# Token mixer of an audio tower: lead of the first scores, order of transfers and adds, and the queue of a third of the stacking transfers

## The chip, the cores and the metric

The kernel runs on one core of a Trainium2 chip. The metric is the device time of one execution in microseconds (us). TensorE, VectorE, ScalarE and GpSimd compute; SyncE and ScalarE also issue the transfers, each on a queue of its own.

## The reference, cut to what matters

The program is a token mixer and two layers of attention and feed-forward. Only the mixer is changed. It is an attention over the 512 time steps of each of 128 sequences, with 32 channels:

```python
q, k, v = jnp.split(qkv, 3, axis=1)                    # 128 sequences, 32 channels, 512 steps
weight = jnp.einsum('bct,bcs->bts', q * scale, k * scale)
weight = jax.nn.softmax(weight.astype(jnp.float32), axis=-1).astype(weight.dtype)
h = jnp.einsum('bts,bcs->bct', weight, v)
```

## The kernel before

The mixer (`token_mixer`, lines 73 to 504) works through 32 tiles of four sequences. Inputs are split into two float16 parts (line 318 on ScalarE, the high part; line 268 on GpSimd, the low part), and stacked in three groups of 32 partitions into `tm_qk`, so that one matmul over 96 rows gives scores of full precision. The stacking is done by transfers within the chip: `stack`, line 207, three for each of the four sequences, on SyncE's queue.

Scores are computed twice. The **first scores** (line 426, bank `tm_s1`, three banks) serve only for the maximum of each row: VectorE reduces them (line 371), and after eight such reductions TensorE transposes the maxima (line 434), VectorE splits them in two float16 rows (lines 381 and 383), and two small transfers (line 214, `maxima`) put these rows under the stacked inputs. The **second scores** (line 446, `tm_s2`, two banks of two) then have the maximum subtracted inside the matmul. ScalarE takes their exponential (line 330, eight for a tile, each over the scores of two places). GpSimd (line 283, three of four sequences) and VectorE (line 397, the last) add halves of the exponentials, TensorE sums these over the rows (line 479, `sum_probs`, into bank 2 of `tm_s1`) and multiplies the exponentials with the values (line 460, `sum_values`). ScalarE copies both out (lines 338 and 344). The sums are brought to a dense shape by a transfer (line 223, `denominators`), inverted on VectorE (line 390), spread again by way of DRAM (lines 230 and 237), and multiplied in on GpSimd (line 275).

All engines follow an order written out by hand. A step n has 16 places g, and at each place TensorE does one first score, of a tile ahead, and one second score of tile n. `LEAD = 15` says how many places the first scores run ahead: at place g stands number g + 15. `MAXIMA_AT` gives the places of the transposes (11 for the first half of the next tile, 3 for the second half of this one; their rows are used at places 0 and 8), `VALUES_AT` those of the four blocks of values (14, and 0, 2, 4 of the next step), `SUMS_AT` those of the two blocks of sums of the tile before (8 and 10). `BANK` names the bank of each use of `tm_s1`: while the sums of a tile hold bank 2, only banks 0 and 1 alternate. Semaphores count each of these; a second score of exponential i waits for exponential i - 2 (`exp_done`), since they share a bank. Steps 4 to 27 are a loop of two steps, the others are written out, the last ones between steps of the attention (`mixer_into_attention`).

Of the kernel before, what the change touches and what calls it, by code (L numbers as in the profile page):

```python
# [72 lines left out]
def token_mixer(nc, sb, ps, sem, qk_dram, vt_dram, ident_dram, rden_dram, h_dram, SEQS=128):  # L73
    C, T = 32, qk_dram.shape[2]
    P = 128
# [11 lines left out]
    LEAD = 15  # L87
# [56 lines left out]
    MAXIMA_AT = {11: 0, 3: 1}  # L144
    VALUES_AT = {14: (0, 0), 0: (1, 1), 2: (1, 2), 4: (1, 3)}
    SUMS_AT = {8: 0, 10: 1}
# [49 lines left out]
    def sync(sp):  # L196
# [3 lines left out]
        def stack(t, u, b):  # L200

            if inside(t, TILES):
                wait_alone(sp, sp_passed, xlo_done, t + 1)
                wait_alone(sp, sp_passed, s2_ready, 8 * (t - 2) + 4 * (b // 2) + 4)
                c = slice(b * C, (b + 1) * C)
                for g, (lo, hi) in enumerate(((0, 2), (0, 3), (1, 2))):
                    sp.dma_start(qk[u][g * C:(g + 1) * C, :, b, :],
                                 xs[u][c, lo:hi + 1:hi - lo, :]).then_inc(stacked[u][b], 16)
# [8 lines left out]

        def denominators(t, u):

            if inside(t, TILES):  # L220
                wait_alone(sp, sp_passed, sums_out, t + 1)
                wait_alone(sp, sp_passed, rden_done, t - 1)
                sp.dma_start(dens[u][:, :], nd[u][0:P:C, 1, :].rearrange("b (a e) -> b a e", e=E))\
                    .then_inc(dens_in[u], 16)
# [18 lines left out]
        def step(k, u):  # L243
            n = 2 * k + u
            stack(n + 1, 1 - u, 2)
            stack(n + 1, 1 - u, 3)
            inverses(n - 2, u, k - 1)
            maxima(n, u, 1)
            inverse_rows(n - 2, u, k - 1)
            stack(n + 2, u, 0)  # L250
            stack(n + 2, u, 1)
            maxima(n + 1, 1 - u, 0)
            denominators(n - 1, 1 - u)
# [10 lines left out]
    def gpsimd(pool):  # L264
# [21 lines left out]
        def step(k, u):  # L286
            n = 2 * k + u
            add(n - 1, 2)
            x_lo(n + 3, 1 - u)
            if not isinstance(n, int) or n < TILES:  # L290
                normalise(n - 2, u, k - 1)
            add(n, 0)
            add(n, 1)
        return step, normalise

    def scalar(act):
        def load(t, u):
            if inside(t, TILES):
                wait_alone(act, act_passed, xlo_done, t - 1)
                act.dma_start(xqk[u][:, :, :], qk_dram[bass.ds(t * P, P)]).then_inc(qk_in[u], 16)  # L300

# [43 lines left out]

        def step(k, u):
            n = 2 * k + u
            for i in range(8):
                exps(n, i)
                if i == 2:  # L350
                    copy_values(n - 1, 1 - u, k + u - 1)
                    load_values(n + 1, 1 - u)
                if i == 3:
                    x_hi(n + 3, 1 - u, k + 1 + u)
                if i == 4:
                    copy_sums(n - 1, 1 - u)
                    load(n + 4, u)
                if i == 6:
                    store(n - 2, u)
        return step, copy_values, copy_sums  # L360

    def vector(dve):
# [37 lines left out]
        def step(k, u):  # L400
            n = 2 * k + u
            for g in range(SLOTS):
# [5 lines left out]
                if g == 1:  # L408
                    inverse_sums(n - 2, u, k - 1)
                if g == 3:  # L410
                    add_last(n - 1)
        return step, inverse_sums, add_last
# [734 lines left out]
def mixer_into_attention(nc, ctx, mixer, att, ternary, down, beside, beside_scalar, beside_vector, beside_tensor,  # L1147
# [66 lines left out]
    def _(act):  # L1214
        mix, copy_values, copy_sums = mixer.scalar(act)
# [21 lines left out]
        copy_sums(31, 1)  # L1237
        run(step, -1, 0)
# [9 lines left out]
    def _(dve):  # L1248
# [14 lines left out]
        inverse_sums(30, 0, 15)  # L1263
        statistics, normalised, low, _, _ = ternary.vector(dve)
        for n in range(1, 34):
            step(n // 2, n % 2, statistics, normalised, low)
            if n == 1:
                inverse_sums(31, 1, 15)
            beside_vector(dve, n)
# [1424 lines left out]
```

## Time and profile before

| what | value |
|---|---|
| median of 3 runs | 2353.75 us (2352.59 to 2357.39) |
| the profiled execution | 2357.19 us, span 2355.4 us |
| granted clock of TensorE, mean | 0.985 of 2.4 GHz |
| busy over the whole span | TensorE 94%, VectorE 71%, ScalarE 65%, GpSimd 54% |
| busy from 100 to 500 us | TensorE 359.3 of 400 us, VectorE 298.0, ScalarE 249.0, GpSimd 253.9; transfer engines 48% |

The mixer takes the first 550 us. Each row of a timeline gives the start of an instruction (or of some alike in a row, x their number), its recorded length, and in brackets how long its engine had been idle and what ended that. Matmuls overlap, so that start to start tells more of TensorE than their length.

### The profile page before, as it was taken

The page shows a single profiled execution, that of the slowest core. Times are in us where ns is not written, and L with a number is a line of the kernel's source. Part 1 is how long each engine was busy: PE and PEld are TensorE (multiplying, and loading weights), DVE is VectorE, ACT ScalarE, POOL GpSimd, SP SyncE. Part 2 cuts the span into 40 slices and gives each one's busy share as a digit, 9 for nine tenths or more (in the row PEclk, how much of TensorE's full clock was granted, in tenths as well). Part 3 has the DMA queues.
Part 4 walks back from the last instruction along what each step waited for, and adds up shares of the span by engine and source line. Part 5 has one row for each costly group of instructions (what it writes and reads, how often), then busy time and mean ns, then how long its engine had stood idle before and what let it go on. Part 6 is the DMA issues. An engine that isn't in the chain of part 4 may idle for free. (4 is left out here: it accounts for less than half of the span.)

```text
span 2355.4 us, 42715 instructions
## 1 busy us (share of the span) xinstructions
PE 2202.6 (94%) x13828; PEld 1076.9 (46%) x13828; DVE 1674.3 (71%) x2922; ACT 1524.0 (65%) x2430; POOL 1266.6 (54%) x1141
## 2 busy tenths in 40 slices
PE   6889889987899998899999999999998999999997
PEld 1222222223566665444444444666664444444443
DVE  6777777774777979666666743666666787788875
ACT  4656666666678779446555522766675777777775
POOL 4566666667677778332324401444444566666654
PEclk9999999998999999899999999999999999999999
DMA  5444454441334222312222212222221011111111
GB/s 147 132 130 133 124 137 125 130 129 38 91 128 132 76 68 68 102 51 79 79 85 85 81 49 72 73 80 79 79 84 46 27 51 50 41 50 41 41 36 63
DMA packets 144049, 194.99 MB, mean 83 GB/s; under 512 B 30469, under 2 KB 73957, under 8 KB 143898
## 3 DMA queue, kind: packets, MB, share of 16 engines
q1 hardware_dynamic: 115866, 154.79, 22.0%
q10 hardware_dynamic: 28032, 38.28, 5.3%
q8 instruction: 84, 1.38, 0.2%
q14 instruction: 67, 0.55, 0.1%
HBM read 125.10 MB, written 42.21 MB: 71 GB/s over the span
## 5 line engine op out<-in xcount | busy, mean ns | idle before, releaser
L2294 PE MATMUL f_bank<-f_xs,gu 128*128 128x512 f16 x1408 | 417.2, 379 | 1.5 <-ACT f_firstg L2120 0.8
L371 DVE TENSOR_REDUCE tm_negmax<-tm_s 128x1 f32<-128x512 f32 x512 | 323.1, 673 | 95.2 <-PE tm_s L426 94.6
L330 ACT ACTIVATE tm_prob<-tm_s 128x1024 f32<-128x1024 f32 x256 | 261.1, 1024 | 192.1 <-PE tm_s L446 173.9
L2322 PE MATMUL f_bank<-dn,f_ghi 128*128 128x512 f16 x704 | 265.6, 379 | 1.9 <-DVE f_glo L2229 1.9
L426 PE MATMUL tm_s<-tm_qk 96*128 96x512 f16 x512 | 200.6, 394 | 47.7 <-DVE tm_negmax L371 27.7
L2084 POOL TENSOR_TENSOR f_firstg<-f_firstg,f_secondg 128x512 f32<-128x512 f32 x88 | 152.2, 1729 | 152.8 <-DVE f_secondg L2213 152.8
L283 POOL TENSOR_TENSOR tm_added<-tm_prob 128x1024 f32<-128x1024 f32 x96 | 223.7, 2355 | 2.3 <-PE tm_s L479 2.2
L446 PE MATMUL tm_s<-tm_qk 98*128 98x512 f16 x512 | 198.0, 389 | 22.6 <-DMA tm_qk<-tm_mrow 19.9
L2294 PEld LDWEIGHTS f_bank<-f_xs,gu 128*128 128x128 f16 x1408 | 136.0, 98 | 162.7 <-ACT f_firstg L2120 1.3
L268 POOL TENSOR_TENSOR tm_xs<-tm_xqk,tm_xs 128x1024 f16<-128x1024 f32 x32 | 68.2, 2130 | 189.9 <-ACT tm_xs L318 189.9
L1048 PE MATMUL a_bankB<-a_wo,a_yThi 128*128 128x512 f16 x512 | 158.7, 393 | 0.0
L2084 POOL TENSOR_TENSOR f_firstu<-f_firstu,f_secondu 128x512 f32<-128x512 f32 x88 | 123.9, 1408 | 64.5 <-DVE f_secondu L2213 64.5
L1088 PE MATMUL a_bankB<-a_wqkv,a_xhi 128*128 128x512 f16 x512 | 154.3, 383 | 0.2
L426 PEld LDWEIGHTS tm_s<-tm_qk 96*128 96x128 f16 x512 | 49.9, 98 | 228.0 <-DVE tm_negmax L371 139.0
L1576 POOL TENSOR_TENSOR fw_value<-fw_value,fw_code 128x512 f32<-128x512 f32 (+1 forms) x35 | 43.8, 1252 | 184.1 <-DVE fw_value L1529 177.3
L460 PE MATMUL tm_o<-tm_prob,tm_vt 128*32 128x512 f32 x1024 | 141.4, 626 | 0.0
L1910 PE MATMUL f_pz<-tern,f_ghi 128*128 128x512 f16 (+1 forms) x352 | 134.4, 382 | 2.9 <-DVE f_glo L1795 2.9
L1910 PE MATMUL f_pz<-tern,f_glo 128*128 128x512 f16 (+1 forms) x352 | 134.2, 381 | 0.0
L2322 PE MATMUL f_bank<-dn,f_glo 128*128 128x512 f16 x352 | 133.4, 379 | 0.0
L698 POOL TENSOR_TENSOR a_qs<-a_qkv,a_qs 128x512 f16<-128x512 f32 x32 | 37.0, 1156 | 171.8 <-ACT a_qs L817 171.8
L748 ACT COPY a_qT<-a_bankD 128x512 f16<-128x512 f16 x128 | 68.6, 587 | 86.2 <-PE a_bankD L1021 86.2
L674 POOL TENSOR_TENSOR a_crossed<-a_qkv,a_sin 128x64 f32<-128x64 f32 (+1 forms) x128 | 80.5, 648 | 73.6 <-ACT a_qkv L787 73.6
(197 smaller groups left out, 5770.1 us busy)
## 6 DMA issues: line engine op xcount, KB each, us to landing
tm_qk<-tm_xs SPq DMA_DIRECT2D x384, 64.0 KB, 2.4
tm_xqk<-in_qk ACTq DMA_DIRECT2D x32, 512.0 KB, 3.8
a_hin<-h SPq DMA_DIRECT2D x64, 256.0 KB, 2.7
a_hres<-h SPq DMA_DIRECT2D x64, 256.0 KB, 3.0
h<-a_hout SPq DMA_DIRECT2D x64, 256.0 KB, 2.5
f_hin<-h SPq DMA_DIRECT2D x64, 256.0 KB, 2.9
f_hres<-h SPq DMA_DIRECT2D x64, 256.0 KB, 2.9
tm_vt<-in_vt ACTq DMA_DIRECT2D x32, 256.0 KB, 6.0
```

The source lines that it names most:

```text
L283: pool.tensor_tensor(added[b][:, :, :], prob[b][:, 0:2, :], prob[b][:, 2:4, :], ALU.add)\
L330: nc.scalar.activation(prob[b][:, 2 * h:2 * h + 2, :], s2[:, i % 2, :, :], ACT.Exp, scale=SCALE).then_inc(exp_done, 1)
L371: nc.vector.tensor_reduce(negmax[u][:, m:m + 1], s1[:, BANK[p], :], AX.X, ALU.max, negate=True).then_inc(s1_read, 1)
L426: nc.tensor.matmul(s1[:, BANK[place(m)], :], qk[u][0:KS, 0, b, i * P:(i + 1) * P], qk[u][0:KS, 1, b, :], start=True, stop=True).then_inc(s ...
L446: last = nc.tensor.matmul(s2[:, i % 2, j, :], qk[u][0:KM, 1, b, s:s + P], qk[u][0:KM, 0, b, :], start=True, stop=True)
L460: last = nc.tensor.matmul(o[C * b:C * (b + 1), :], vt[u][:, j, :, b], prob[b][:, j, :], start=j == 0, stop=j == NT - 1)
L1048: last = nc.tensor.matmul(bankB[:, :], a, w[:, r, :], start=n == 0, stop=n == 3 * R - 1)
L1088: last = nc.tensor.matmul(out, a[u][:, j, :], w[:, j, cols], start=n == 0, stop=n == 3 * KT - 1)
L1910: last = nc.tensor.matmul(pz[i % 2][:, :], gparts[x][u][0:rows[m], m, i * P:(i + 1) * P], down[0:rows[m], m, :], start=c == 0, stop=c == 2 ...
L2084: pool.tensor_tensor(to[:, :], to[:, :], other[:, :], ALU.add).then_inc(s["sum_done"], 1)
L2294: last = nc.tensor.matmul(bank_of(m, i)[:, :], (gate, up)[which][:, j, m * P:(m + 1) * P], xs[g % 2][:, x, j, :], start=x == 0, stop=x == 1)
L2322: last = nc.tensor.matmul(pz[i][:, :], gparts[x][:, (MT * g + m) % RING, i * P:(i + 1) * P], down[w][:, m, :], start=m == 0 and c % 3 == 0 ...
```

## The change

- `LEAD` goes from 15 to 17. The transposes move with it, from places 11 and 3 to 9 and 1, the sums from places 8 and 10 to 5 and 7; VectorE's add (line 397) goes from behind place 3 to behind place 2, and its reciprocal (line 390) from place 1 of the step after next to place 14 of the next.
- The third stacking transfer of each sequence (`stack_last`) is issued by ScalarE: those of two sequences behind the first exponential of a step, those of two behind the fifth.
- The transfer of the denominators is issued by ScalarE too, right behind the copy of the sums, which moves from behind the fifth exponential to behind the fourth. The high part of the inputs (`x_hi`, line 318) moves from behind the fourth to behind the fifth.
- GpSimd makes the low part of the inputs (`x_lo`) at the end of a step and no longer before its multiplication and two adds.
- SyncE's order is a new one, below. At the end of the mixer the last denominators and reciprocals follow the new order.

```diff
-    LEAD = 15
+    LEAD = 17
...
-    MAXIMA_AT = {11: 0, 3: 1}
+    MAXIMA_AT = {9: 0, 1: 1}
     VALUES_AT = {14: (0, 0), 0: (1, 1), 2: (1, 2), 4: (1, 3)}
-    SUMS_AT = {8: 0, 10: 1}
+    SUMS_AT = {5: 0, 7: 1}
...
-                for g, (lo, hi) in enumerate(((0, 2), (0, 3), (1, 2))):
+                for g, (lo, hi) in enumerate(((0, 2), (0, 3))):
...
             n = 2 * k + u
             stack(n + 1, 1 - u, 2)
+            inverse_rows(n - 2, u, k - 1)
+            maxima(n, u, 1)
             stack(n + 1, 1 - u, 3)
-            inverses(n - 2, u, k - 1)
-            maxima(n, u, 1)
-            inverse_rows(n - 2, u, k - 1)
             stack(n + 2, u, 0)
+            maxima(n + 1, 1 - u, 0)
             stack(n + 2, u, 1)
-            maxima(n + 1, 1 - u, 0)
-            denominators(n - 1, 1 - u)
+            inverses(n - 1, 1 - u, k + u - 1)
...
             add(n - 1, 2)
-            x_lo(n + 3, 1 - u)
             if not isinstance(n, int) or n < TILES:
                 normalise(n - 2, u, k - 1)
             add(n, 0)
             add(n, 1)
+            x_lo(n + 3, 1 - u)
...
+        def stack_last(t, u, b):
+
+            if inside(t, TILES):
+                wait_alone(act, act_passed, xlo_done, t + 1)
+                wait_alone(act, act_passed, s2_ready, 8 * (t - 2) + 4 * (b // 2) + 4)
+                c = slice(b * C, (b + 1) * C)
+                act.dma_start(qk[u][2 * C:3 * C, :, b, :], xs[u][c, 1:3, :]).then_inc(stacked[u][b], 16)
...
             for i in range(8):
                 exps(n, i)
+                if i == 0:
+                    stack_last(n + 1, 1 - u, 2)
+                    stack_last(n + 1, 1 - u, 3)
+                if i == 4:
+                    stack_last(n + 2, u, 0)
+                    stack_last(n + 2, u, 1)
                 if i == 2:
                     copy_values(n - 1, 1 - u, k + u - 1)
                     load_values(n + 1, 1 - u)
                 if i == 3:
+                    copy_sums(n - 1, 1 - u)
+                    denominators(n - 1, 1 - u)
+                if i == 4:
                     x_hi(n + 3, 1 - u, k + 1 + u)
-                if i == 4:
-                    copy_sums(n - 1, 1 - u)
+                if i == 5:
                     load(n + 4, u)
-                if i == 6:
                     store(n - 2, u)
...
                 maxes(n + ahead, (u + ahead) % 2, m)
-                if g == 1:
-                    inverse_sums(n - 2, u, k - 1)
-                if g == 3:
+                if g == 2:
                     add_last(n - 1)
+                if g == 14:
+                    inverse_sums(n - 1, 1 - u, k + u - 1)
```

ScalarE, a step behind its third exponential, before. `tm_prob` are the exponentials, `tm_nd` the copies of values and sums:

```order
30 L338 COPY tm_nd<-tm_o 128x512
31 L306 DMA tm_vt<-in_vt 128x4x128
32 L330 ACTIVATE tm_prob<-tm_s 128x1024
33 L318 CAST tm_xs<-tm_xqk 128x2x512
34 L330 ACTIVATE tm_prob<-tm_s 128x1024
35 L344 COPY tm_nd<-tm_s 128x512
36 L300 DMA tm_xqk<-in_qk 128x1024
37 L330 ACTIVATE tm_prob<-tm_s 128x1024 x2
38 L165 DMA h<-tm_nd 128x512
39 L330 ACTIVATE tm_prob<-tm_s 128x1024
```

And now, the same stretch, with the lines of the changed kernel:

```order
43 L337 COPY tm_nd<-tm_o 128x512
44 L305 DMA tm_vt<-in_vt 128x4x128
45 L329 ACTIVATE tm_prob<-tm_s 128x1024
46 L343 COPY tm_nd<-tm_s 128x512
47 L350 DMA tm_dens<-tm_nd 128x1x16
48 L329 ACTIVATE tm_prob<-tm_s 128x1024
49 L299 DMA tm_qk<-tm_xs 32x2x512 x2
50 L317 CAST tm_xs<-tm_xqk 128x2x512
51 L329 ACTIVATE tm_prob<-tm_s 128x1024
52 L291 DMA tm_xqk<-in_qk 128x1024
53 L165 DMA h<-tm_nd 128x512
54 L329 ACTIVATE tm_prob<-tm_s 128x1024 x2
```

The cast (318, now 317) stood between the exponentials of the long places and now stands behind two stacking transfers (299); the copy of the sums and the denominators' transfer (350) now come ahead of it.

TensorE from the second block of sums on, before, with what each instruction waits for (`tm_s1_read`: a bank read by VectorE; `tm_exp_done`: exponentials):

```order
119 L479 MATMUL tm_s<-tm_added,tm_ones 32x512 x4
120 L434 MATMUL tm_s<-tm_ident,tm_negmax 8x128 [waits tm_s1_read]
121 L426 MATMUL tm_s<-tm_qk 128x512 [waits tm_s1_read]
122 L446 MATMUL tm_s<-tm_qk 128x512
123 L426 MATMUL tm_s<-tm_qk 128x512 [waits tm_sums_out,tm_s1_read]
124 L446 MATMUL tm_s<-tm_qk 128x512 [waits tm_exp_done]
125 L426 MATMUL tm_s<-tm_qk 128x512 [waits tm_s1_read,tm_stacked13]
126 L446 MATMUL tm_s<-tm_qk 128x512
127 L426 MATMUL tm_s<-tm_qk 128x512 [waits tm_s1_read]
128 L446 MATMUL tm_s<-tm_qk 128x512 [waits tm_exp_done]
129 L460 MATMUL tm_o<-tm_prob,tm_vt 32x512 [waits tm_exp_done,tm_values_out,tm_v_in0]
130 L460 MATMUL tm_o<-tm_prob,tm_vt 32x512 x3
```

And now (line 440 is a first score, 460 a second, 448 the transpose, 493 a block of sums):

```order
115 L493 MATMUL tm_s<-tm_added,tm_ones 32x512 x4
116 L440 MATMUL tm_s<-tm_qk 128x512 [waits tm_s1_read]
117 L460 MATMUL tm_s<-tm_qk 128x512 [waits tm_exp_done,tm_mrow_in1]
118 L448 MATMUL tm_s<-tm_ident,tm_negmax 8x128 [waits tm_s1_read]
119 L440 MATMUL tm_s<-tm_qk 128x512 [waits tm_s1_read]
120 L460 MATMUL tm_s<-tm_qk 128x512
121 L440 MATMUL tm_s<-tm_qk 128x512 [waits tm_sums_out,tm_s1_read]
122 L460 MATMUL tm_s<-tm_qk 128x512 [waits tm_exp_done]
123 L440 MATMUL tm_s<-tm_qk 128x512 [waits tm_s1_read,tm_stacked13]
124 L460 MATMUL tm_s<-tm_qk 128x512
125 L440 MATMUL tm_s<-tm_qk 128x512 [waits tm_s1_read]
126 L460 MATMUL tm_s<-tm_qk 128x512 [waits tm_exp_done]
```

Before, four places (11 to 14) lie between the second block of sums and the next block of values; now seven (8 to 14, of which the rows show six and the values come after the seventh). The transpose now stands behind the first of them.

## Rows read from the trace of the kernel before

**Rows 1.** Waits from 100 to 560 us: engine and line that waited <- released by: us, times, longest.
```profile
PE tm_s L426 <- DVE tm_negmax L371: 22.5, 26, 2.1
PE tm_s L446 <- DMA tm_qk<-tm_mrow: 17.4, 23, 2.3
```
**Rows 2.** Timeline, ScalarE (start, length, operation): copy of values, first and last of 24 tiles.
```profile
111.46 0.58 ACT L338 COPY tm_nd<-tm_o 128x512 f32<-128x512 f32 x1
...
487.53 0.58 ACT L338 COPY tm_nd<-tm_o 128x512 f32<-128x512 f32 x1
```
**Rows 3.** Timeline, TensorE, one tile: start us, length, operation, [idle before it <- releaser].
```profile
317.98 1.10 PE L460 MATMUL tm_o<-tm_prob,tm_vt 128*32 128x512 f32 x8
319.01 0.39 PE L426 MATMUL tm_s<-tm_qk 96*128 96x512 f16 x1
...
324.98 0.39 PE L426 MATMUL tm_s<-tm_qk 96*128 96x512 f16 x1 [0.83 <-DVE tm_negmax L371]
...
325.81 0.38 PE L446 MATMUL tm_s<-tm_qk 98*128 98x512 f16 x1
326.12 1.06 PE L479 MATMUL tm_s<-tm_added,tm_ones 128*32 128x512 f32 x8
327.12 0.39 PE L426 MATMUL tm_s<-tm_qk 96*128 96x512 f16 x1
327.34 0.38 PE L446 MATMUL tm_s<-tm_qk 98*128 98x512 f16 x1
...
329.09 0.27 PE L434 MATMUL tm_s<-tm_ident,tm_negmax 128*8 128x128 f32 x1
329.20 0.38 PE L426 MATMUL tm_s<-tm_qk 96*128 96x512 f16 x1
...
334.00 0.39 PE L446 MATMUL tm_s<-tm_qk 98*128 98x512 f16 x1 [0.69 <-DMA tm_qk<-tm_mrow]
```
**Rows 4.** Timeline, ScalarE, the same tile (ACTq: it issues a transfer).
```profile
326.55 1.04 ACT L318 CAST tm_xs<-tm_xqk 128x1024 f16<-128x1024 f32 x1
327.84 1.02 ACT L330 ACTIVATE tm_prob<-tm_s 128x1024 f32<-128x1024 f32 x1 [0.26 <-PE tm_s L446]
329.22 0.58 ACT L344 COPY tm_nd<-tm_s 128x512 f32<-128x512 f32 x1 [0.36 <-PE tm_s L479]
329.53 0.35 ACTq L300 DMA_DIRECT2D tm_xqk<-in_qk  x1
330.05 1.99 ACT L330 ACTIVATE tm_prob<-tm_s 128x1024 f32<-128x1024 f32 x2 [0.24 <-PE tm_s L446]
```
**Rows 5.** Timeline, VectorE, the same tile.
```profile
323.66 3.06 DVE L371 TENSOR_REDUCE tm_negmax<-tm_s 128x1 f32<-128x512 f32 x5
...
327.54 1.29 DVE L371 TENSOR_REDUCE tm_negmax<-tm_s 128x1 f32<-128x512 f32 x2 [0.82 <-PE tm_s L426]
```
**Rows 6.** Timeline, SyncE's queue: a pair of row transfers, six stacking transfers.
```profile
330.17 1.45 SPq L214 DMA_DIRECT2D tm_qk<-tm_mrow  x2
...
333.19 4.03 SPq L207 DMA_DIRECT2D tm_qk<-tm_xs  x6
```
**Rows 7.** Issues by line, whole program: ns min/median/max, first and last start us.
```profile
L207 SPq DMA_DIRECT2D tm_qk<-tm_xs x384: 585/597/1772, 7.9 to 516.9; - x192
L306 ACTq DMA_DIRECT2D tm_vt<-in_vt x32: 375/395/701, 8.7 to 520.0; - x32
```
**Rows 8.** Timeline, GpSimd, one tile.
```profile
327.66 2.13 POOL L268 TENSOR_TENSOR tm_xs<-tm_xqk,tm_xs 128x1024 f16<-128x1024 f32 x1 [5.45 <-ACT tm_xs L318]
```
**Rows 9.** Timeline, TensorE: longer waits in other tiles, and a matmul behind the first.
```profile
122.14 0.60 PE L446 MATMUL tm_s<-tm_qk 98*128 98x512 f16 x1 [2.31 <-DMA tm_qk<-tm_mrow]
...
124.54 0.61 PE L426 MATMUL tm_s<-tm_qk 96*128 96x512 f16 x1
...
351.04 0.39 PE L446 MATMUL tm_s<-tm_qk 98*128 98x512 f16 x1 [1.57 <-DMA tm_qk<-tm_mrow]
...
522.43 0.39 PE L426 MATMUL tm_s<-tm_qk 96*128 96x512 f16 x1 [2.08 <-DVE tm_negmax L371]
```

More of the change, by code:

```diff
@@ L216, in maxima @@
                                  mrow[pair][:, part, :]).then_inc(mrow_in[pair], 16)
[L218 to L224, printed above, removed]
         def inverses(t, u, half):
@@ L344, in copy_sums, with denominators @@
                 nc.scalar.copy(nd[u][:, 1, :], sums_bank(t)).then_inc(sums_out, 1)
+        def denominators(t, u):
+            if inside(t, TILES):
+                wait_alone(act, act_passed, sums_out, t + 1)
+                wait_alone(act, act_passed, rden_done, t - 1)
+                act.dma_start(dens[u][:, :], nd[u][0:P:C, 1, :].rearrange("b (a e) -> b a e", e=E))\
+                    .then_inc(dens_in[u], 16)
         def step(k, u):
@@ L353, in step @@
                 if i == 3:
+                    copy_sums(n - 1, 1 - u)
+                    denominators(n - 1, 1 - u)
+                if i == 4:
                     x_hi(n + 3, 1 - u, k + 1 + u)
-                if i == 4:
-                    copy_sums(n - 1, 1 - u)
+                if i == 5:
                     load(n + 4, u)
-                if i == 6:
                     store(n - 2, u)
-        return step, copy_values, copy_sums
+        return step, copy_values, copy_sums, denominators
     def vector(dve):
@@ L1214, in _ @@
     def _(act):
-        mix, copy_values, copy_sums = mixer.scalar(act)
+        mix, copy_values, copy_sums, denominators = mixer.scalar(act)
         prepare, step = att.scalar(act)
@@ L1237, in _ @@
         copy_sums(31, 1)
+        denominators(31, 1)
         run(step, -1, 0)
@@ L1262, in _ @@
         run(step, -2, 0)
-        inverse_sums(30, 0, 15)
+        inverse_sums(31, 1, 15)
         statistics, normalised, low, _, _ = ternary.vector(dve)
@@ L1266, in _ @@
             step(n // 2, n % 2, statistics, normalised, low)
-            if n == 1:
-                inverse_sums(31, 1, 15)
             beside_vector(dve, n)
```

## The prediction

> **What bounds the kernel now.** I read the busy shares by stage first, then who waited for whom, then the timeline of one tile of the token mixer on each engine. All that changes lies in that mixer. In its steady stretch TensorE is busy some 90% of the time, ScalarE 62%, VectorE 75%, GpSimd 64% (the table above), so TensorE is the engine whose waits count. Of those two stand out [rows 1]: a first score (line 426) that waits for VectorE's maximum to free its bank, 22.5 us in 26 waits, and a second score (line 446) that waits for the small transfers of row maxima, 17.4 us in 23 waits. Rows of that list are the recorded idle time only; the tile's timeline gives the whole loss.
>
> A step has 16 places. From the same copy in 24 successive steps [rows 2]: (487.53 - 111.46) / 23 = 16.35 us a step. What TensorE needs for a step without waits [rows 3]: a place holds two matmuls 0.22 apart (327.12 to 327.34), so 0.44; a block of values adds 0.31 + 1.03 (317.98 to 319.01) less 0.22, so 1.12; a block of sums 0.31 + 1.00 less 0.22, so 1.09; a transpose 0.11 (329.09 to 329.20). The sum is 16 x 0.44 + 4 x 1.12 + 2 x 1.09 + 2 x 0.11 = 13.92 us. So 2.4 us a step are waits, and over 28 steady steps 68 us at most could be had.
>
> **The change part by part.** Times below count from the start of line 426 at place 0.
>
> *Two places more lead.* The transposes move from places 11 and 3 to 9 and 1, their users stay at 0 and 8: each row of maxima has 7 places to land where it had 5. In the tile shown it was 0.69 us late at place 0 [rows 3]; two light places are 0.88. The longest such wait was 2.31 [rows 9]. The second wait, 0.83 at place 7, came because VectorE made its own add just before (five reductions back to back, 3.06 us [rows 5]) while places 5 to 7 were short ones. After the change VectorE's add stands at place 2, among long places. Both waits go. The work of filling and draining the pipeline moves by two reductions, 2 x 0.61 us at the start, won back at the end: nothing.
>
> *What is late next.* Blocks now stand at places 0, 2, 4 (values), 5, 7 (sums) and 14 (values). Places 0 to 7 take 8 x 0.44 + 3 x 1.12 + 2 x 1.09 + 0.11 = 9.17 us. Then come six short places in a row, 8 to 13, where there were at most three. There bank 2 is lent to the sums, so only two banks alternate: place 9 needs the reduction of place 8. It starts 0.42 after its matmul (327.12 to 327.54), takes 0.63, and the bank is seen free 0.08 later (third reduction's start 323.66 + 2 x 0.61 = 324.88, second's end 324.90, matmul 324.98) [rows 3, 5]. So place 9 starts at 9.17 + 0.42 + 0.63 + 0.08 = 10.30 and not at 9.72: 0.58 us. Its second score is at 10.52, and the fifth exponential starts 0.50 behind (327.34 to 327.84) [rows 3, 4]: 11.02.
>
> *ScalarE's queue.* It gets five more issues a step: four stacking transfers and the one of denominators. An issue holds ScalarE's program: in the tile shown the load is issued from 329.53 for 0.35, and the next exponential starts at 330.05, 0.17 after it ended, as it does in other tiles [rows 4]. Issues behind the first exponential (0.31 + 1.29 + 0.17 = 1.77 us) fit before the second, 2 us later. The denominators' issue follows the copy of the sums (0.58, from 0.13 after the sums' end, 329.09 to 329.22) and waits for it: 9.17 + 0.13 + 0.58 + 0.17 + 0.60 = 10.65, before 11.02, so it is hidden. The two behind the fifth exponential are not, because the cast of the inputs (line 318, 1.04 us) follows them, and moved from the long places to just here. The nearest price of one is the same transfer on SyncE's queue, 0.597 median [rows 7], six in 4.03 us, so 0.09 between two [rows 6]. The cast starts at 11.02 + 0.31 + 0.60 + 0.09 + 0.60 + 0.17 = 12.79; the sixth exponential 1.0 later, 13.8, ends at 14.82. Place 14's second score waits for it (they share a bank of second scores): 14.90, where TensorE alone would be at 12.14 + 0.58 = 12.72. Then a block of values, 0.31 + 1.03, and place 15, 0.44: the step is 16.68 us long.
>
> Bounds of that price: from below the cheapest issue on ScalarE's queue, 0.35 [rows 4], which gives 16.18. From above an issue there while SyncE issues too: line 306 takes 0.395 and at worst 0.701 [rows 7], at 8.7 us, beside stacking transfers. SyncE's row transfers (1.45 us a pair) are issued 1.08 after their transpose (329.09 to 330.17 [rows 3, 6]), so from 10.7 at the earliest, with VectorE's reduction of place 8 ahead of its part some 10.9 to 12.4: beside the two of ScalarE's. With 0.31 more for each the step is 17.30. I add half of one, 0.15, since one overlaps wholly and the other in part: **16.83 us**.
>
> The Trainium skill (Perfetto Trace Analysis, DMA Instruction — HWDGE) says that both sequencers share one descriptor generator, and that waiting for its lock is inside the recorded issue. The longest issue of line 306 agrees with that; taken for both issues it gives the upper bound, 17.30.
>
> *SyncE, GpSimd, VectorE.* SyncE loses four of twelve stacking issues and the denominators' one, 5 x 0.60 = 3 us a step. It had room: between a pair of row transfers (to 331.62) and the next six issues (from 333.19) lie 1.57 us [rows 6], of which the denominators' took some 0.60. GpSimd's low parts move behind its two adds, in the time in which it stood idle for 5.45 us before the cast [rows 8]; its third add then ends some 2 us into the next step, where the sums want it at 5.9. The sums' earlier places need VectorE's add, over by 4.9, also in time. If either slipped by a place it would cost 0.44. The reciprocals now run at place 14, where VectorE waits anyway. Nothing for these.
>
> **Sum.** (16.83 - 16.35) x 28 = +13.4 us. The profiled execution took 2357.2 (span 2355.4), 3.4 over the median of the runs, 2353.75. The difference goes on the median: **2367 us**, slower. Without the added 0.15: +9; bounds of the issue alone: -5 to +27.
>
> **The rivals.** *Faster: the issues don't hold ScalarE.* If they are hidden behind the exponential, the cast follows at 11.02 + 0.97, the last score at 14.1, and the step is 15.88: -13 us, 2340.5. For it: all waits on rows of maxima end, and with them single ones of 1.57 and 2.31 us [rows 9]. Against: the 0.17 behind the load's issue. The Trainium skill (Trainium Kernel Development and Optimization, Key Constraints) says that issuing from several engines saves the sequencer's issue time only; here SyncE's was not on the path.
>
> *No change: losses meet gains.* With 0.40 for an issue, as line 306's median, the step is 16.28: -2 us, 2352.
>
> *Slower by more: the clock falls in the new gap.* TensorE will idle from about 13.2 to 14.9 in each step, 1.7 us, behind short waits. Before, it ran at 2.4 GHz after 1.57 and 2.08 us idle, but after 2.31 us matmuls took 0.60 (1.2 GHz) and the next first score came 2.40 us later where it should be 1.34 [rows 9]: 1.1 us lost, up to 1.5 with what follows. In half the steps that adds 14 x 1.1 to 14 x 1.5 = 15 to 21 us: 2382 to 2388. It decides once the gap exceeds some 2 us.
>
> *The change doesn't do what it says:* the order of instructions shows that it does; I give this no chance of its own.
>
> **Numbers.** A change under 0.2%, 4.7 us, can't be told from none here. Chances: the forecast 0.44 (2358 to 2380, for an issue of 0.5 to 0.9), the clock 0.16 (2380 to 2395), no change 0.14, faster 0.26 (down to 2340). Range 2340 to 2390: beyond it lie the clock falling in nearly every step, and GpSimd or VectorE freed to more than I see. Faster 0.26, same 0.14, slower 0.60.
>
> **What would show it.** Right: the step of copies near 16.8; TensorE waits at place 14 for line 329's exponential (line 330 before), 1.5 us or more, hardly ever for the row transfers, and 0.2 to 0.6 at place 9 for VectorE; each cast starts 1.7 us or more after the exponential. Wrong: a cast within 1.1 us of it, an issue of line 299 near 0.35, or a step below 16.1. For the clock: matmuls of 0.6 behind place 14 in many steps.

## The result, and the profile after

| | us |
|---|---|
| before, median of 4 runs | 2354.47 (2352.59 to 2357.39) |
| changed, median of 4 runs | 2389.24 (2386.29 to 2396.72) |
| ratio | 1.0151, 95% interval 1.0123 to 1.0179 |
| the profiled execution, changed | 2386.29, span 2384.3, granted clock 0.981 |

The change costs 34.8 us by the medians and 29.1 us by the two profiled executions (2386.29 against 2357.19). The forecast had the sign, and its range (2340 to 2390) holds the time, though by less than 1 us at its upper end; for the size it had +13.4 us.

The page of the changed kernel, its parts on the engines and on the queues, and the same stretch by windows as in the table of before (PE, PEld, DVE, ACT and POOL busy, granted clock, share of the transfer engines, GB/s):

```profile
PE 2213.5 (93%) x13828; PEld 1076.0 (45%) x13828; DVE 1677.6 (70%) x2922; ACT 1523.1 (64%) x2430; POOL 1268.7 (53%) x1141
...
q1 hardware_dynamic: 101402, 146.13, 20.1%
q10 hardware_dynamic: 42496, 46.94, 7.1%
```
```profile
100.00:500.00 400.00, 340.40 (x1830) 87.14 (x1829) 279.24 (x496) 226.61 (x249) 233.48 (x114) 0.96 0.44 118
```

Transfers have gone from SyncE's queue (q1, 22.0% of the transfer engines' time before) to ScalarE's (q10, 5.3% before), as meant. Every engine does less in the same 400 us: TensorE is busy for 340.4 us, not 359.3, and its mean clock there is 0.96, not 1.00. Nothing has become a busier engine; waits have grown, and part of the work ran at the lower clock.

Waits of TensorE from 100 to 560 us, the counterpart of [rows 1]:

```profile
PE tm_s L460 <- ACT tm_prob L329: 47.3, 26, 2.0
PE tm_s L440 <- DVE tm_negmax L385: 13.0, 28, 0.5
PE tm_s L440 <- DMA tm_qk<-tm_xs: 4.9, 9, 1.4
```

The two waits of [rows 1] are gone or halved: no row for the transfers of row maxima is left, and VectorE's 22.5 us are 13.0. In their place stands one on ScalarE's exponential, 47.3 us in 26 steps, and a new small one, on a stacking transfer.

Timeline of ScalarE, the copy of values (line 337, 338 before), five of 23, as in [rows 2]:

```profile
100.01 0.58 ACT L337 COPY tm_nd<-tm_o 128x512 f32<-128x512 f32 x1
...
245.60 0.58 ACT L337 COPY tm_nd<-tm_o 128x512 f32<-128x512 f32 x1
...
264.04 0.58 ACT L337 COPY tm_nd<-tm_o 128x512 f32<-128x512 f32 x1
...
280.87 0.58 ACT L337 COPY tm_nd<-tm_o 128x512 f32<-128x512 f32 x1
...
492.46 0.58 ACT L337 COPY tm_nd<-tm_o 128x512 f32<-128x512 f32 x1
```

The 22 steps between the first and the last take (492.46 - 100.01) / 22 = 17.84 us, 1.49 more than the 16.35 of before. But they are not alike. One takes 264.04 - 245.60 = 18.44 us, the next 280.87 - 264.04 = 16.83. Ten of the 22 lie between 18.3 and 19.9 (mean 18.77), twelve between 16.8 and 17.5 (mean 17.07).

Timeline of TensorE for another step of the shorter kind (17.37 us, since it has a wait at place 7), with its three waits (places 7, 9 and 14):

```profile
315.85 0.39 PE L440 MATMUL tm_s<-tm_qk 96*128 96x512 f16 x1 [0.31 <-DMA tm_qk<-tm_xs]
...
318.56 0.39 PE L440 MATMUL tm_s<-tm_qk 96*128 96x512 f16 x1 [0.46 <-DVE tm_negmax L385]
...
323.31 0.39 PE L460 MATMUL tm_s<-tm_qk 98*128 98x512 f16 x1 [1.91 <-ACT tm_prob L329]
323.63 1.09 PE L474 MATMUL tm_o<-tm_prob,tm_vt 128*32 128x512 f32 x8
```

Timeline of ScalarE beside it, from the fifth exponential on, the counterpart of [rows 4]:

```profile
319.29 1.02 ACT L329 ACTIVATE tm_prob<-tm_s 128x1024 f32<-128x1024 f32 x1 [1.18 <-PE tm_s L460]
319.54 1.43 ACTq L299 DMA_DIRECT2D tm_qk<-tm_xs  x2
321.29 1.05 ACT L317 CAST tm_xs<-tm_xqk 128x1024 f16<-128x1024 f32 x1 [0.98 <-PE tm_s L460]
...
322.24 1.02 ACT L329 ACTIVATE tm_prob<-tm_s 128x1024 f32<-128x1024 f32 x1
```

The chain reads off directly. The fifth exponential starts at 319.29; its two issues run to 320.97; the cast starts 0.32 after that, at 321.29, though ScalarE had been idle for 0.98 us; the sixth exponential follows at 322.24 and ends at 323.26; TensorE's second score of place 14 starts at 323.31 after 1.91 us without work. (The releaser "PE tm_s L460" of the cast is only the last semaphore seen; the cast reads nothing of TensorE. What held it are the issues.)

In a step of the longer kind the matmuls behind that gap are slow. Timeline of TensorE, the step that took 18.44 us:

```profile
253.39 0.39 PE L460 MATMUL tm_s<-tm_qk 98*128 98x512 f16 x1 [1.90 <-ACT tm_prob L329]
253.71 1.94 PE L474 MATMUL tm_o<-tm_prob,tm_vt 128*32 128x512 f32 x8
255.58 0.61 PE L440 MATMUL tm_s<-tm_qk 96*128 96x512 f16 x1
```

The block of values takes 1.94 us instead of the 1.09 at 323.63, a single matmul 0.61 instead of 0.39: the clock is at its lower level, 1.2 GHz, from 253.71 to about 257. From the gap's end to the next transpose the shown slow step takes 4.89 us (253.39 to 258.28) and an undisturbed one 3.35 (305.95 to 309.30): 1.54 us lost. There are eleven such stretches from 127 to 520 us in the mixer, where the kernel before had two in its loop, at 122 and 504 us.

### The profile page after: what moved, and what is told of

Its sections match the earlier page's. It is cut to its first block and busy times, and to the rows that moved or that the text cites. A ratio compares the mean times of both kernels' runs of the same rounds, so it can differ in the third digit from the quotient of the medians.

```text
span 2384.3 us, 42979 instructions
## 1 busy us (share of the span) xinstructions
PE 2213.5 (93%) x13828; PEld 1076.0 (45%) x13828; DVE 1677.6 (70%) x2922; ACT 1523.1 (64%) x2430; POOL 1268.7 (53%) x1141
## 5 line engine op out<-in xcount | busy, mean ns | idle before, releaser
L385 DVE TENSOR_REDUCE tm_negmax<-tm_s 128x1 f32<-128x512 f32 x512 | 328.3, 682 | 137.4 <-PE tm_s L440 134.3
L460 PE MATMUL tm_s<-tm_qk 98*128 98x512 f16 x512 | 201.8, 396 | 60.5 <-ACT tm_prob L329 57.9
L440 PE MATMUL tm_s<-tm_qk 96*128 96x512 f16 x512 | 206.3, 405 | 35.1 <-DMA tm_qk<-tm_xs 17.7
L474 PE MATMUL tm_o<-tm_prob,tm_vt 128*32 128x512 f32 x1024 | 150.6, 663 | 0.0
L266 POOL TENSOR_TENSOR tm_nd<-tm_nd,tm_rows 128x512 f32<-128x512 f32 x32 | 40.8, 1273 | 181.0 <-DMA tm_rows<-rden 181.0
```

The source lines that it names most:

```text
L385: nc.vector.tensor_reduce(negmax[u][:, m:m + 1], s1[:, BANK[p], :], AX.X, ALU.max, negate=True).then_inc(s1_read, 1)
L440: nc.tensor.matmul(s1[:, BANK[place(m)], :], qk[u][0:KS, 0, b, i * P:(i + 1) * P], qk[u][0:KS, 1, b, :], start=True, stop=True).then_inc(s ...
L460: last = nc.tensor.matmul(s2[:, i % 2, j, :], qk[u][0:KM, 1, b, s:s + P], qk[u][0:KM, 0, b, :], start=True, stop=True)
L474: last = nc.tensor.matmul(o[C * b:C * (b + 1), :], vt[u][:, j, :, b], prob[b][:, j, :], start=j == 0, stop=j == NT - 1)
```

## The experiments

Two theories at first. **A:** ScalarE's chain (fifth exponential, two issues, cast, sixth exponential) makes the gap at place 14, and the gap lets the clock fall. **B:** stacking transfers through two queues land later or disturb others, whatever ScalarE does. A third, **C:** the earlier sums and the longer lead cost time by themselves.

**The cast put back ahead (cast_back).** It runs again behind the fourth exponential, before the copy of the sums; all else as changed.

```diff
                 if i == 3:
+                    x_hi(n + 3, 1 - u, k + 1 + u)
                     copy_sums(n - 1, 1 - u)
                     denominators(n - 1, 1 - u)
                 if i == 4:
-                    x_hi(n + 3, 1 - u, k + 1 + u)
```

> The changed kernel with the cast of the inputs moved back from behind the fifth exponential (and its two stacking issues) to behind the fourth, ahead of the copy of the sums. Theory A (ScalarE's chain of fifth exponential, two issues, cast, sixth exponential holds place 14, and TensorE's clock falls in about half of the gaps this makes): the chain loses the cast, some 0.9 us; a step goes from 17.3 to 16.4 us where the clock holds, the gap at place 14 from 1.9 to about 1.0 us, the clock falls in at most two steps, and the time is 2345 to 2358 us. Theory B (the stacking transfers land later because two queues and the spread of the inverses share the transfer engines): the loss is at place 7 and stays, 2375 us or more. Theory C (the earlier sums and the longer lead cost by themselves, through the two banks): 2375 us or more.

Measured: 2370.76 us (2365.8 to 2374.78), ratio 1.0065 (1.0043 to 1.0087). 18 us better than the change, but 13 worse than I expected under A. Waits of TensorE, 100 to 560 us:

```profile
PE tm_s L459 <- ACT tm_prob L329: 35.4, 48, 0.8
...
PE tm_s L439 <- ACT tm_nd L343: 2.6, 6, 0.8
```

The one long wait has become two of at most 0.8 us a step, and of the eleven stretches at the lower clock five are left. That part of A holds. But the two waits add up to 35.4 / 24 = 1.5 us a step where 1.0 was expected, because the sixth exponential still has to wait for the two issues (it starts 1.88 us behind the fifth in the tile at 312.46). What was not foreseen is the last row, the copy of the sums, which is now late; and the waits for stacking transfers are 8.4 us in 9, up from 4.9.

**All stacking back on SyncE (on_sync).** The new order stays, ScalarE's four stacking issues go.

```diff
-                for g, (lo, hi) in enumerate(((0, 2), (0, 3))):
+                for g, (lo, hi) in enumerate(((0, 2), (0, 3), (1, 2))):
...
-                if i == 0:
-                    stack_last(n + 1, 1 - u, 2)
-                    stack_last(n + 1, 1 - u, 3)
-                if i == 4:
-                    stack_last(n + 2, u, 0)
-                    stack_last(n + 2, u, 1)
```

> The changed kernel with all three stacking transfers of a sequence on SyncE's queue again, the rest of its order kept. Theory A: the two issues (1.44 us and 0.3 behind them) go from ahead of the cast, the cast starts 0.95 us behind the fifth exponential instead of 2.0; place 14's wait falls from 1.9 to about 0.9 us, the clock holds, a step is 16.0 to 16.4 us and the time 2335 to 2355 us. Theory B: place 7's wait for stacking transfers goes too; if that alone goes, a step is shorter by 0.3 to 0.5 us and the time 2375 to 2382 us. Theory C: no change beyond 5 us, 2384 to 2394 us.

Measured: 2332.88 us (2331.99 to 2335.32), ratio 0.9914 (0.9895 to 0.9933): 56 us under the changed kernel and 22 under the kernel before, 2 us better than the range expected under A. Its step is 15.80 us in 22 steps running. The end of the gap on TensorE, then ScalarE's chain:

```profile
324.50 0.39 PE L454 MATMUL tm_s<-tm_qk 98*128 98x512 f16 x1 [0.81 <-ACT tm_prob L329]
```
```profile
321.57 1.02 ACT L329 ACTIVATE tm_prob<-tm_s 128x1024 f32<-128x1024 f32 x1 [1.18 <-PE tm_s L454]
322.49 1.04 ACT L317 CAST tm_xs<-tm_xqk 128x1024 f16<-128x1024 f32 x1
```

The cast starts 0.92 after the exponential instead of 2.00, the gap is 0.81 us, and no stretch at the lower clock is left in the loop. C falls with it: order, lead and sums' places are those of the change, and they gain 22 us.

**Both (both_back).** Cast ahead and stacking on SyncE, to see if the two repairs add up.

```diff
                 if i == 3:
+                    x_hi(n + 3, 1 - u, k + 1 + u)
                     copy_sums(n - 1, 1 - u)
...
-                    stack_last(n + 2, u, 0)
-                    stack_last(n + 2, u, 1)
```

> Both edits together: stacking all on SyncE, cast behind the fourth exponential; what is left of the change is the lead of 17, the earlier transposes and sums, the orders of SyncE, GpSimd and VectorE, and the denominators on ScalarE. Theory A: nothing but the sixth exponential itself follows the fifth, place 14 waits 0.5 us or less, a step is 15.0 to 15.6 us and the time 2318 to 2338 us, faster than both kernels. Theory B: as with stacking on SyncE alone. Theory C: not under 2354 us.

Measured: 2355.51 us (2344.21 to 2364.88), ratio 0.9998 (0.9978 to 1.0017). A miss: 23 us worse than on_sync alone. ScalarE and TensorE in one of the long steps:

```profile
331.64 1.04 ACT L317 CAST tm_xs<-tm_xqk 128x1024 f16<-128x1024 f32 x1 [0.77 <-DMA tm_qk<-tm_xs]
332.59 0.58 ACT L343 COPY tm_nd<-tm_s 128x512 f32<-128x512 f32 x1
```
```profile
333.31 0.38 PE L433 MATMUL tm_s<-tm_qk 96*128 96x512 f16 x1 [0.79 <-ACT tm_nd L343]
```

The cast overwrites the tile from which stacking transfers still read, so it waits for them to land; behind it on ScalarE stands the copy that gives bank 2 back, and for that TensorE waits: 12.1 us in 12 waits. Waits of the two engines, 100 to 560 us:

```profile
PE tm_s L433 <- ACT tm_nd L343: 12.1, 12, 2.1
```
```profile
ACT tm_xs L317 <- DMA tm_qk<-tm_xs: 13.0, 12, 3.2
```

So the cast's place is bounded from both sides. Behind the fourth exponential it is too early for the transfers, and behind the fifth with issues ahead of it too late for the sixth. Cast_back has the same waits of the cast, 3.1 us in 7, which is part of why it gained less than A said.

The waits alone are not the 23 us, though. Of the 24 steps from 98 to 494 us, the 13 without a wait for the copy take 15.4 to 15.5 us, less than the 15.80 of on_sync. Of the 11 with one, four take 16.0 to 16.4 us and seven 17.4 to 19.4 (mean 18.58), and in those seven the clock falls. TensorE in one of them:

```profile
233.77 0.38 PE L433 MATMUL tm_s<-tm_qk 96*128 96x512 f16 x1 [1.01 <-ACT tm_nd L343]
...
234.54 0.63 PE L453 MATMUL tm_s<-tm_qk 98*128 98x512 f16 x1
```

From there matmuls take 0.6 us up to 241.1. The falls cost 7 x (18.58 - 16.29) = 16 us, the larger part of the miss. And no wait of nearly 2 us stands ahead of them: in six of the seven steps the longest wait is 1.1 us or less, behind another of 0.46 at place 9. What separates them from the four steps with like waits and no fall stays open.

**A gap filled with work (gap_filled).** The first score of place 14 is computed seven times instead of once, so that some 1.3 us of the gap are busy.

```diff
+                for _ in range(6 if m == SLOTS - 1 else 0):
+                    nc.tensor.matmul(s1[:, BANK[place(m)], :], qk[u][0:KS, 0, b, i * P:(i + 1) * P],
+                                     qk[u][0:KS, 1, b, :], start=True, stop=True)
                 nc.tensor.matmul(s1[:, BANK[place(m)], :], qk[u][0:KS, 0, b, i * P:(i + 1) * P],
```

> The changed kernel with the first score of place 14 computed seven times over (the same matmul into the same bank, the last one counts), so that TensorE works for 1.3 us of the 1.9 in which it waits at place 14. The wait itself is not shortened. Theory A, its part on the clock: no stretch of 0.6 us matmuls behind place 14 in the mixer, where the changed kernel has eleven; at 1.1 to 1.3 us each the time falls by 10 to 15 us, to 2374 to 2380. If the clock were not what makes half of the steps 1.1 us longer, they stay so and the time is 2387 to 2392.

Measured: 2371.58 us (2370.26 to 2372.78), ratio 1.0075 (1.0056 to 1.0094). TensorE does 6 matmuls more in each step and the kernel is 17.7 us quicker than the changed one, somewhat more than the 10 to 15 expected. No slow stretch is left in the loop. This prices the clock apart from the gap: the second score of place 14 comes no sooner (3.97 us behind the fifth exponential's start in the tile at 327.38, 4.02 in that at 319.29 of the changed kernel), the chain on ScalarE is the same, and half of the loss goes.

**The queue alone (queue_only).** The kernel before, in its own order, with the third stacking transfers on ScalarE behind the first and the fifth exponential.

```diff
                 exps(n, i)
+                if i == 0:
+                    stack_last(n + 1, 1 - u, 2)
+                    stack_last(n + 1, 1 - u, 3)
+                if i == 4:
+                    stack_last(n + 2, u, 0)
+                    stack_last(n + 2, u, 1)
```

> The kernel before with nothing changed but the queue: the third stacking transfer of a sequence is issued by ScalarE, two behind the first exponential of a step and two behind the fifth. Theory A: behind the fifth exponential stands the copy of the sums; the two issues (1.44 us) push it 0.5 to 0.6 us later, TensorE waits that much longer at place 12, and the sixth exponential comes later too: +0.5 us in each of 28 steps, 2364 to 2374 us, the clock holds. If ScalarE's issues hurt only where the cast follows them, the time is 2350 to 2358 us.

Measured: 2356.14 us (2348.72 to 2360.71), ratio 1.0004 (0.999 to 1.0018). A miss: it costs nothing there. Waits of TensorE, 100 to 560 us:

```profile
PE tm_s L440 <- DVE tm_negmax L385: 21.1, 26, 1.3
PE tm_s L460 <- DMA tm_qk<-tm_mrow: 10.4, 22, 0.8
PE tm_s L440 <- ACT tm_nd L352: 6.3, 14, 0.5
```

In the order of before the cast stands ahead of the fifth exponential, and behind the issues there comes only the copy of the sums, for which TensorE waits up to 0.5 us (third row). That wait was expected; the loss was not there. The waits for row maxima shrink from 17.4 us [rows 1] to 10.4, though SyncE issues them no sooner behind the transpose (a median of 1.09 us in both traces). The wait for the copy stands between the transpose and the use of its rows, so that part of one wait may have taken the place of the other; this was not tried. The same transfers on the same queue cost nothing measurable here and 56 us in the new order.

**One issue instead of two (one_issue).** Of the pair behind the fifth exponential one goes back to SyncE.

```diff
                 if i == 4:
                     stack_last(n + 2, u, 0)
-                    stack_last(n + 2, u, 1)
```

> The changed kernel with one stacking issue behind the fifth exponential instead of two (that of the second sequence goes back to SyncE). Theory A: a dose. The cast starts 0.72 us earlier, place 14 waits 1.15 to 1.25 us instead of 1.9 (0.8 with none), and the clock falls in two steps at most: a step of 16.6 us where it was 17.3, and the time 2350 to 2362 us, nearer to the 2333 of none than to the 2389 of two. If it were the place of the cast alone or the sharing of queues as such, the wait would stay near 1.9 and the time above 2380 us.

Measured: 2352.65 us (2350.53 to 2356.1), ratio 0.9997 (0.9986 to 1.0008). The gap, in a typical step:

```profile
320.71 0.39 PE L459 MATMUL tm_s<-tm_qk 98*128 98x512 f16 x1 [1.07 <-ACT tm_prob L329]
...
331.18 0.39 PE L439 MATMUL tm_s<-tm_qk 96*128 96x512 f16 x1 [0.87 <-DMA tm_qk<-tm_xs]
```

From two issues to one the gap shrinks by 0.84 us, from one to none by 0.26, since most of one fits beside the exponential that ScalarE is running. At 1.07 us of gap two stretches at the lower clock are left, one at 93 us and one of 3.6 us from 471.8; the second stands in a step with waits of 0.67 and 1.12 us. The wait at place 7 (second row) stays.

**The rows of inverses later (rows_later).** That wait at place 7 is for a stacking transfer of ScalarE's first pair, issued 0.4 us behind the spread of the inverses (256 KB). Here this spread is issued behind the row maxima and the fourth stacking.

```diff
-            inverse_rows(n - 2, u, k - 1)
             maxima(n, u, 1)
             stack(n + 1, 1 - u, 3)
+            inverse_rows(n - 2, u, k - 1)
```

> The changed kernel with SyncE issuing the spread of the inverses (256 KB, the largest transfer on its queue) behind the maxima and the fourth sequence's stacking, and no longer ahead of them. Theory A takes the 0.3 to 1.4 us that place 7 waits for a stacking transfer for a transfer issued by ScalarE 0.4 us behind that spread, in line with it on the transfer engines: the wait at place 7 goes, 0.3 to 0.5 us a step, 2372 to 2382 us. Theory B (two queues by themselves make stacking land late): the wait stays, 2386 to 2392 us. A risk is the multiplication on GpSimd, which comes 3 us later and could hold back its adds.

Measured: 2401.52 us (2400.86 to 2404.82), ratio 1.0204 (1.0183 to 1.0226). A miss. Timeline of GpSimd:

```profile
303.91 1.26 POOL L266 TENSOR_TENSOR tm_nd<-tm_nd,tm_rows 128x512 f32<-128x512 f32 x1 [9.53 <-DMA tm_rows<-rden]
```

GpSimd waits 9.53 us for the spread, where the changed kernel waits 5.3 to 7.2 (median 6.1), and its adds and the low parts, from which all stacking is fed, are queued behind. What that costs shows on VectorE, whose add now falls together with one of GpSimd. Timelines of VectorE and of TensorE in another tile:

```profile
221.30 2.76 DVE L411 TENSOR_TENSOR tm_added<-tm_prob 128x1024 f32<-128x1024 f32 x1
```
```profile
224.72 0.39 PE L440 MATMUL tm_s<-tm_qk 96*128 96x512 f16 x1 [1.27 <-DVE tm_negmax L385]
```

The add takes 2.76 us with 1.68 us of it beside GpSimd's add, where it takes 1.20 in the changed kernel, always with GpSimd idle. The reductions behind it are late, and TensorE's waits for them rise from 13.0 to 19.9 us (longest 1.3). Stretches at the lower clock rise from 11 to 15. On the suspected cost itself theory A was right: no wait for a stacking transfer is left, and ScalarE's 90 from 100 to 510 us land 2.0 to 2.6 us after their issue, where those of the changed kernel take up to 6.4. The run traded that cost for a larger one.

**The two pairs apart (first_sync, fifth_sync).** first_sync puts the pair behind the first exponential back on SyncE, fifth_sync the other. With the changed kernel and on_sync they make a square of four.

```diff
-                for g, (lo, hi) in enumerate(((0, 2), (0, 3))):
+                for g, (lo, hi) in enumerate(((0, 2), (0, 3)) + (((1, 2),) if b > 1 else ())):
...
-                if i == 0:
-                    stack_last(n + 1, 1 - u, 2)
-                    stack_last(n + 1, 1 - u, 3)
```

In fifth_sync it is `if b < 2`, and the two lines behind the fifth exponential go:

```diff
-                if i == 4:
-                    stack_last(n + 2, u, 0)
-                    stack_last(n + 2, u, 1)
```

> The changed kernel, with the two third stacking transfers behind the first exponential back on SyncE's queue; the two behind the fifth stay on ScalarE's. If the chain behind the fifth exponential and the clock falls in its gap are nearly the whole loss, the gap at place 14 stays 1.8 to 1.9 us, with some 10 stretches of slow matmuls, and the time is 2370 to 2390. If the late transfer at place 7 comes from the pair on ScalarE's queue behind the first exponential, the wait there (up to 1.4 us, some 0.5 a step) goes, worth 10 to 15 us by itself: 2370 to 2378, and steps without a clock fall of 16.7 to 16.9 us instead of 17.0 to 17.4. If it is the other pair, or the rows of inverses, the wait stays and the time is 2382 to 2390.

> The other half: the two behind the fifth exponential back on SyncE's queue, those behind the first stay on ScalarE's. The gap at place 14 shrinks to 0.8 us and no slow matmuls follow it. If the loss is the chain and the clock, the time is 2332 to 2345, as with all on SyncE (2332.9), and with the place 7 wait kept 2340 to 2347. If two queues of stacking transfers by themselves cost (the rival), it stays above 2355.

| median, us | fifth pair on ScalarE | fifth pair on SyncE |
|---|---|---|
| **first pair on ScalarE** | 2389.24 (changed) | 2347.25 (fifth_sync) |
| **first pair on SyncE** | 2379.57 (first_sync) | 2332.88 (on_sync) |

Ratios to before: first_sync 1.0097 (1.0079 to 1.0116), fifth_sync 0.997 (0.9959 to 0.998). The fifth pair costs 42.0 or 46.7 us, the first 9.7 or 14.4. Waits of TensorE for first_sync, then for fifth_sync, 100 to 560 us:

```profile
PE tm_s L457 <- ACT tm_prob L329: 47.1, 26, 1.9
```
```profile
PE tm_s L457 <- ACT tm_prob L329: 23.4, 27, 2.0
...
PE tm_s L437 <- DMA tm_qk<-tm_xs: 9.1, 18, 0.9
```

Each pair has its own wait: the fifth pair the one on the exponential, the first pair the one on the stacking transfer, 9.1 us in 18 waits where it stands on ScalarE and no row where it doesn't. Why it is late shows in the order of issues. The changed kernel, ScalarE's queue and SyncE's:

```profile
310.55 1.48 ACTq L299 DMA_DIRECT2D tm_qk<-tm_xs  x2
```
```profile
308.01 1.26 SPq L207 DMA_DIRECT2D tm_qk<-tm_xs  x2
310.14 0.60 SPq L229 DMA_DIRECT2D tm_rows<-rden  x1
```

And first_sync, SyncE's queue:

```profile
301.13 1.90 SPq L207 DMA_DIRECT2D tm_qk<-tm_xs  x3
303.39 0.60 SPq L229 DMA_DIRECT2D tm_rows<-rden  x1
```

On SyncE the third transfer of a sequence goes out with the other two, ahead of the spread. On ScalarE it has to wait for the first exponential to be started, 2.5 us behind the first of them, and goes out after the spread. The time from issue to landing of the changed kernel's two from 310.55, then the page's row on all such transfers of that queue, with its median:

```profile
DMA to landing us min/median/max: 3.1/4.2/5.2
...
tm_qk<-tm_xs ACTq DMA_DIRECT2D x128, 64.0 KB, 2.4
```

One of the two lands 5.2 us after its issue, at some 315.8, and TensorE goes on at 315.85; the median is 2.4. Of the two differences, the later issue and the spread ahead of it, rows_later keeps the first and takes away the second, and there all land within 2.6 us and nothing waits for them. In the changed kernel itself the second pairs, with no spread just ahead, land in 2.0 to 2.5 us, the first pairs in 2.5 to 6.4. So it is the spread ahead of them that makes them late. Theory B, two queues as such, is left with nothing but this: fifth_sync has both queues and takes 2347 us.

**The cast behind the sixth exponential (cast_late).** A version drawn from all this: on_sync with the cast one exponential later, off the path to place 14.

```diff
-                if i == 4:
-                    x_hi(n + 3, 1 - u, k + 1 + u)
                 if i == 5:
+                    x_hi(n + 3, 1 - u, k + 1 + u)
                     load(n + 4, u)
```

> A version to beat both: stacking all on SyncE (2333 us) and the cast behind the sixth exponential, where TensorE's block of values at place 14 covers it, not ahead of it. Theory A: the sixth exponential comes 0.93 us earlier, the wait at place 14 of 0.81 us goes to nearly nothing, a step is 14.9 to 15.2 us instead of 15.80, and the time is 2312 to 2324 us. If something else held the step (GpSimd's low part, which starts 1 us later, or the stacking behind it), it stays above 2328 us.

Measured: 2319.77 us (2317.87 to 2323.6), ratio 0.986 (0.9838 to 0.9881): 35 us under the kernel before, the best here. ScalarE's timeline:

```profile
360.21 1.94 ACT L329 ACTIVATE tm_prob<-tm_s 128x1024 f32<-128x1024 f32 x2 [1.18 <-PE tm_s L453]
...
362.03 1.05 ACT L317 CAST tm_xs<-tm_xqk 128x1024 f16<-128x1024 f32 x1
```

The fifth and the sixth exponential now run back to back, and the cast falls into the long places. The time is as expected; steps take 14.9 to 15.5 us, two of them 16.1.

## Why the prediction was right and wrong

**Which waits go: right.** The waits for row maxima and the 0.83 us at place 7 for VectorE went as said. On_sync shows what the new order is worth by itself: 15.80 against 16.35 us a step.

**What is late next: right.** From place 8 to place 9 the forecast has 10.30 - 9.17 = 1.13 us; in the tile shown place 8 starts at 317.39 and place 9 at 318.56, 1.17.

**ScalarE's queue, the term on which the forecast rests: right in size.** It said 16.83 us for a step. Undisturbed steps of the changed kernel without a wait at place 7 take 16.83 (that from 264.04 to 280.87, for one), and first_sync, where they are free of the place 7 wait as well, has its undisturbed ones at 16.83 to 16.92. The chosen 0.60 for an issue is 0.63 by the 128 issues (0.592 to 0.774):

```profile
L299 ACTq DMA_DIRECT2D tm_qk<-tm_xs x128: 592/627/774, 8.1 to 558.5; - x128
```

The forecast put the cast 1.77 us behind the exponential and 0.15 more for the overlap; it is 2.00 here, and 1.95 in the tile before. The 0.15 was right for another reason than the one given: the two issues take 0.63 and 0.60 us, as on SyncE, but 0.20 passes between them (0.09 assumed) and 0.32 between the second and the cast (0.17 assumed). The upper bound, 0.31 more for each issue beside SyncE's, did not show, though SyncE issued its pair of row transfers from 319.10 to 320.53, beside both. That forecast and trace agree to 0.01 us is therefore in part luck. Issued from ScalarE the transfer costs its program 0.6 us even though ScalarE's arithmetic runs on. For the rival "the issues don't hold ScalarE" nothing is left; on_sync is what it would have looked like, and its step of 15.80 is near the 15.88 given to that rival.

**The step that failed first: the clock as a rival of 0.16.** "In half the steps that adds 14 x 1.1 to 14 x 1.5 = 15 to 21 us", with the condition that the gap "exceeds some 2 us". Both the number of steps and the price were close: 10 of 22 steps, (18.77 - 17.07) = 1.70 us each, so 0.77 a step on average, 0.77 x 28 = 22 us; gap_filled won 17.7 us by ending it. Wrong was the condition. The threshold was drawn from three single waits, 1.57 and 2.08 us without a fall and 2.31 with one. The trace of the kernel before had a fourth that speaks against it, a wait of 1.79 us with a fall right behind. Timeline of TensorE:

```profile
504.09 0.39 PE L426 MATMUL tm_s<-tm_qk 96*128 96x512 f16 x1 [1.79 <-DVE tm_negmax L371]
...
504.69 0.61 PE L426 MATMUL tm_s<-tm_qk 96*128 96x512 f16 x1
```

So the clock fell after 1.79 us and did not after 2.08: the length of a single wait doesn't decide it. Gaps of 1.85 to 1.91 us, one in each step behind some six short places, let the clock fall in about half the steps of the changed kernel, and both_back has falls behind waits of 1.1 us or less. The clock belonged in the sum: with it the forecast would have been 2382 to 2388, and 2389.24 was measured.

**The step that failed second: "Nothing for these".** The stacking transfers were counted as issues on both queues, but not followed to the matmul that reads them. Two places more lead ask for the third sequence of the next tile two places earlier, and on ScalarE its last part goes out later. What makes it late is the spread issued ahead of it, as rows_later shows. The undisturbed mean of 17.07 over 16.83 makes this 0.24 us a step, 0.24 x 28 = 7 us; the square gives 9.7 to 14.4 us.

**A gain that was not seen.** 0.48 for the chain, 0.24 and 0.77 add up to the measured 1.49 a step, 42 us for 28 steps; but the profiled executions are 29 apart. At the fourth tile from the end the copy of values is 44.0 us later than before, and the last one starts 35.4 us later (552.82 before, 588.19 now): 8.6 us come back in the mixer's last three steps. Another 6.4 come back behind it. Timeline of TensorE there, in the kernel before, with the longer of two such waits (2.88 and 1.50 us); the changed kernel waits 0.20 us at most in their places:

```profile
594.57 0.63 PE L1078 MATMUL a_bankA<-a_ident,a_xn 128*128 128x128 f32 x4 [2.88 <-DVE a_yTlo L966]
```

On_sync gains about as much behind the mixer (19.1 us at the last copy, 24.9 in the span), and all other kernels in the new order 5.4 to 8.5 us, but queue_only nothing (6.1 and 5.9). It therefore belongs to the new order and not to the queue; what in the order does it was not tried.

**"No change" and the forecast's own case** had the mechanism in common and differed in an issue's price; the price was settled above.

## What to carry to other kernels

- A transfer issued from a computing engine's queue is an instruction of that engine: price it by what stands behind it in program order and by who waits for that. The same four issues cost nothing measurable in the old order and 56 us in the new one.
- When a change makes one wait of nearly 2 us in every step, put the fall of TensorE's clock into the sum; a few single waits of the old trace give no safe threshold, and here falls also followed waits of 1.1 us or less. Filling such a gap with useless matmuls, if it can't be closed, won back half the loss here.
- If the first users of a transfer move earlier, follow every transfer that feeds them from issue to landing, look for a large one issued just ahead of it, and give an instruction that overwrites a source of transfers the latest place that its own user allows.

## What the runs showed of the hardware that was not expected

- **The clock's cost differs from run to run.** The four runs of the changed kernel have a mean granted clock of 0.982, 0.981, 0.978 and 0.975 and take 2386.6, 2386.3, 2391.9 and 2396.7 us; the two with the lower clock are the longer ones. On_sync, with gaps of 0.81 us, lies within 3.3 us.
- **Falls come in a pattern.** In first_sync steps of 19.7 and 18.4 us come in pairs, with three of 16.8 to 16.9 between them in most of the stretch (16.90, 16.84, 16.90, 19.68, 18.46). All have nearly the same gap (1.84 to 1.94 us). What sets the pattern stays open.
- **A fall can last longer than one block.** In first_sync the step of 19.72 us has its gap at 315.96 and matmuls of 0.6 us up to 322.1, with two blocks of values of 1.94 us each among them; it loses 2.8 us. The stretches of the changed kernel last 3.2 to 3.7 us; the one shown of both_back lasts 6.9 (234.2 to 241.1).
- **VectorE's add grows beside GpSimd's.** In rows_later the add of line 411 takes 1.20 us in the ten tiles where no add of GpSimd runs at the same time, and more with each part of it that does: 1.25 with 0.17 us in common, 2.07 with 0.99, 2.76 with 1.68.
